# A graph network on one core: node map stored first with records of 8 words, softmax segments of 7 groups with a shorter order, and the norm product moved beside the bias product

## The reference, cut to what matters

```python
h = relu(layernorm(x))
for m in range(3):                       # block 1: attention, each node also has an edge to itself
    z = h @ W[m]; e = leaky(z[src] @ a_src[m] + z[dst] @ a_dst[m])
    w = exp(e - segment_max(e, dst)); alpha = w / segment_sum(w, dst)
    h = h + sigmoid(segment_sum(alpha * z[src], dst) + bias[m])
x = x + h
h = relu(layernorm(x)); ea = None
for l in range(3):                       # block 2: edge network
    ea = relu(concat(h[src], h[dst], ea) @ We[l] + be[l])
    h = relu(concat(h, segment_sum(ea * norm, dst)) @ Wn[l] + bn[l])
x = x + h
```

## Time and profile before

| | us |
|---|---|
| median of 3 runs | 6682.43 |
| lowest, highest | 6681.06, 6689.92 |
| profiled execution, its own time | 6695.05 |
| its span, first to last instruction | 6693.5 |
| PE busy | 4940.3 (74%) |
| DVE busy | 4362.5 (65%) |
| POOL busy | 4258.7 (64%) |
| ACT busy | 3640.2 (54%) |
| mean granted clock of PE | 0.875 |

### The profile page before, as it was taken

One profiled execution on the slowest core, in us unless ns is written; L12 is line 12 of the kernel. 1 busy time (PEld: TensorE's weight loads), 2 busy tenths in 40 slices (PEclk: granted clock), 3 DMA queues, 4 the chain that ended last, 5 costly groups with the idle time before them and its releaser, 6 DMA issues. The chain is left out here.

```text
span 6693.5 us, 109612 instructions
## 1 busy us (share of the span) xinstructions
PE 4940.3 (74%) x23142; PEld 2996.6 (45%) x23142; DVE 4362.5 (65%) x12362; ACT 3640.2 (54%) x7966; POOL 4258.7 (64%) x4317
## 2 busy tenths in 40 slices
PE   2999999999984527855782567149989997776665
PEld 1566556655651114423441445036656664333332
DVE  4887788777866747856883789855545554444443
ACT  2898889888875726643672344753323332333332
POOL 2777777777830177737745774047766665777777
PEclk9999999999998958876896555579999999999998
DMA  5788888777754536645662788877767775444442
GB/s 159 256 275 276 265 280 273 251 235 227 231 190 162 184 110 203 205 132 162 207 215 87 214 241 250 264 214 215 215 195 230 228 227 166 135 135 133 129 131 92
DMA packets 887891, 1338.57 MB, mean 200 GB/s; under 512 B 285987, under 2 KB 342895, under 8 KB 880915
## 3 DMA queue, kind: packets, MB, share of 16 engines
q1 hardware_dynamic: 744730, 1095.06, 49.2%
q0 software_dynamic: 142688, 238.37, 14.7%
HBM read 676.09 MB, written 662.90 MB: 200 GB/s over the span
## 5 line engine op out<-in xcount | busy, mean ns | idle before, releaser
L1298 POOL DMA_INDIRECT g_xs<-table,g_gi x1176 | 1205.5, 1025 | 988.9 <-DMA g_gi<-in_src_lookups_dram 404.1
L1626 POOL DMA_INDIRECT n_xs<-table,n_gi x1176 | 1202.4, 1022 | 813.7 <-DMA n_gi<-lookups 470.8
L1767 DVE TENSOR_TENSOR_SCAN n_dT<-n_km,n_dT,bank 128x512 f32<-128x512 uint8 x291 | 372.5, 1280 | 1053.5 <-PE bank L1654 1025.1
L1727 ACT ACTIVATE n_eT<-bank,edge_b 128x512 f32<-128x512 f32 x294 | 202.1, 688 | 805.4 <-PE bank L1671 805.4
L693 PE MATMUL bank<-n_zT,wn 128*128 128x512 f32 (+1 forms) x1176 | 542.7, 597 | 84.3 <-ACT n_sg L751 61.3
L674 PE MATMUL bank<-n_xT,gat_w 128*128 128x512 f32 (+1 forms) x1176 | 561.4, 615 | 54.1 <-issue 35.7
L1174 DVE CUSTOM_DVE_ANT_0 g_junk<-g_xs,v_src 128x128 f32<-128x128 f32 x1176 | 276.1, 289 | 486.8 <-DMA g_xs<-table,g_gi 486.2
L1637 POOL DMA_INDIRECT out_dram<-n_xn,n_eo x392 | 426.6, 1088 | 129.8 <-issue 114.9
L1365 PE MATMUL bank<-ident,g_xw 128*128 128x128 f32 x1176 | 240.6, 340 | 332.6 <-DVE g_acc L1193 274.7
L609 POOL DMA_INDIRECT p_rows<-in_x_dram,p_es x392 | 395.6, 1009 | 124.7 <-issue 112.3
L614 POOL DMA_INDIRECT node_map<-p_es x392 | 398.6, 1017 | 119.5 <-issue 113.4
(11 more groups left out here) (253 smaller groups left out, 12263.3 us busy)
## 6 DMA issues: line engine op xcount, KB each, us to landing
table<-n_ro SPq DMA_DIRECT2D x768, 256.0 KB
g_gb<-decays SPq DMA_DIRECT2D x294, 256.0 KB, 4.3
n_xd<-table SPq DMA_DIRECT2D x294, 256.0 KB
table<-g_xn SPq DMA_DIRECT2D x196, 256.0 KB
g_xo<-table SPq DMA_DIRECT2D x196, 256.0 KB, 4.7
edge_feats<-n_eT SPq DMA_DIRECT2D x196, 256.0 KB, 2.8
table<-n_xn SPq DMA_DIRECT2D x196, 256.0 KB, 3.1
n_ea<-edge_feats SPq DMA_DIRECT2D x196, 256.0 KB
```

The source lines that it names most:

```text
L1298: q.indirect_dma_start(out=xs[g % XR][:, u, :], out_offset=None, in_=tables[l], in_offset=bass.IndirectOffsetOnAxis(ap=gi[g % 6][:, 0, u:u ...
L1626: q.indirect_dma_start(out=xs[g][:, u, :], out_offset=None, in_=tables[L], in_offset=bass.IndirectOffsetOnAxis(ap=gi[g][:, u, slot_word:sl ...
L1767: V.tensor_tensor_scan(in_order(dT[g][:, :]), kept(g), in_order(flat_banks[1]), 0.0 if begins(g) else carry(dT[g.before(1)]), ALU.mult, AL ...
```

## The change

- Setup: records and map rows have 8 words instead of 16. DVE clears only the unused words of the records. SP issues the edge loads without waiting for DVE, except for one that loads into a tile that DVE clears first; the first node numbers are loaded ahead of them under a semaphore of their own. DVE makes the map before it takes up the edge rows, and SP stores it after the constants and before the zero rows.
- Attention layers: segments of 7 groups; two softmax functions share a step where each had one, in another order within the step; everything behind the softmax has a lag smaller by 10; XR is 20; three buffers for ACT's half sum.
- Edge layers: the norm product is a function of its own. In layers 0 and 1 it stands between `enter` and `nodes`; in layer 2 it stays behind `edges`.

```diff
@@ -27,14 +27,14 @@
 MR = UN // MG
-SG = 14
+SG = 7
 assert MAPP * MAPN == N and TP * TU == TAIL and BP * BJ == NB and BP <= P and (NM - 1) * P * MU + LP * MU == N and LP <= P and GE % SG == 0
...
 SLOPE = 0.2
-NF = 16
+NF = 8
 MW = NF
@@ -221,6 +221,7 @@
         s_mc = sem("map_cleared")
+        s_nl = sem("node_numbers_loaded")
         s_st = sem("setup_stored")
@@ -267,7 +268,7 @@
             edge_loads = [(edge_i[:, :, :], edges), (wcol[:, :], edge_w), (slots[:, :], slot_numbers),
-                          (row_i[:, :], dst_rows.rearrange("g u e -> g (u e)")), (first_numbers[:, :], node_numbers),
+                          (row_i[:, :], dst_rows.rearrange("g u e -> g (u e)")),
                           (before_i[1:GE, :], dst_rows[0:GE - 1, U - 1, P - 1:P])]
@@ -282,15 +283,28 @@
 
+                    do(V.memset(before_i[:, :].bitcast(f32), -1.0))
+                    mark["cleared"] = n[0]
                     do(V.memset(ones3[:, :], 1.0))
-                    do(V.memset(rec[:, :, :], 0.0))
+                    do(V.memset(rec[:, :, LASTM + 1:NF], 0.0))
                     do(V.memset(keep8[:, :], 0.0))
...
                     do(V.memset(negs[:, :], 0.0))
-                    do(V.memset(before_i[:, :].bitcast(f32), -1.0))
                     do(V.memset(open_first[:, :], 0.0))
                     do(V.memset(nothing[:, :, :], 0.0))
-                    mark["cleared"] = n[0]
+                    mark["unused"] = n[0]
+                    v.wait_ge(s_nl, 16)
+                    do(V.tensor_scalar(numbers[:, 0:1], first_numbers[0:MAPP, 0:1], float(MAPN // U),
+                                       -float(NODE0 * (MAPN // U - 1)), ALU.mult, ALU.add))
+                    seen()
+                    for k in range((MAPN - 1).bit_length()):
+                        m = min(1 << k, MAPN - (1 << k))
+                        do(V.tensor_scalar(numbers[:, 1 << k:(1 << k) + m], numbers[:, 0:m], float(1 << k), None, ALU.add))
+                        seen()
+                    v.wait_ge(s_mc, 1)
+                    for k in MAPPED:
+                        do(V.tensor_copy(map_rows[:, :, k], numbers[:, :]))
+                    mark["map"] = n[0]
                     v.wait_ge(s_el, 16 * len(edge_loads))
@@ -340,8 +354,6 @@
                     do(V.tensor_copy(rec_i[:, :, LASTS], slots[:, :]))
-                    do(V.tensor_scalar(numbers[:, 0:1], first_numbers[0:MAPP, 0:1], float(MAPN // U),
-                                       -float(NODE0 * (MAPN // U - 1)), ALU.mult, ALU.add))
                     seen()
@@ -359,15 +371,6 @@
                     mark["records"] = n[0]
-
-                    for k in range((MAPN - 1).bit_length()):
-                        m = min(1 << k, MAPN - (1 << k))
-                        do(V.tensor_scalar(numbers[:, 1 << k:(1 << k) + m], numbers[:, 0:m], float(1 << k), None, ALU.add))
-                        seen()
-                    v.wait_ge(s_mc, 1)
-                    for k in MAPPED:
-                        do(V.tensor_copy(map_rows[:, :, k], numbers[:, :]))
-                    mark["map"] = n[0]
 
@@ -433,13 +436,17 @@
                 def _(sp):
-                    sp.wait_ge(s_dv, mark["cleared"])
+                    sp.dma_start(first_numbers[:, :], node_numbers).then_inc(s_nl, 16)
                     for to, of in edge_loads[:-1]:
                         sp.dma_start(to, of).then_inc(s_el, 16)
+                    sp.wait_ge(s_dv, mark["cleared"])
                     with nc.allow_non_contiguous_dma("last destination of each row"):
...
                         sp.dma_start(to, of).then_inc(s_cl, 16)
+                    sp.wait_ge(s_dv, mark["map"])
+                    sp.dma_start(node_map.rearrange("(p n) w -> p n w", p=MAPP), map_rows[:, :, :]).then_inc(s_st, 16)
+                    sp.wait_ge(s_dv, mark["unused"])
                     for l in range(1, 2 * LAYERS):
@@ -455,8 +462,6 @@
                                  rec[:, :, :].rearrange("p (g u) f -> p g (u f)", u=U)).then_inc(s_st, 16)
-                    sp.wait_ge(s_dv, mark["map"])
-                    sp.dma_start(node_map.rearrange("(p n) w -> p n w", p=MAPP), map_rows[:, :, :]).then_inc(s_st, 16)
                     sp.wait_ge(s_st, 16 * (2 * LAYERS + 7))
@@ -974,7 +979,7 @@
             ends = [(S_ + 1) * SG - 1 for S_ in range(GE // SG)]
-            XR, OR = 28, 9
+            XR, OR = 20, 9
             ix, gx = sems(f"g{l}_indices_loaded", 6), sems(f"g{l}_gathered", XR)
@@ -994,7 +999,7 @@
                 xw, acc = of_ring(f"g{l}_xw", 3, c=c2), of_ring(f"g{l}_acc", 3, (C, U * P), c=c2)
-                th, xh, xn = of_ring(f"g{l}_th", 2, c=c2), of_ring(f"g{l}_xh", 2, c=c2), of_ring(f"g{l}_xn", 4, c=c2)
+                th, xh, xn = of_ring(f"g{l}_th", 2, c=c2), of_ring(f"g{l}_xh", 3, c=c2), of_ring(f"g{l}_xn", 4, c=c2)
                 xr = of_ring(f"g{l}_xr", 4, c=c2) if last_layer else None
@@ -1203,7 +1208,7 @@
                             V.scalar_tensor_tensor(out=xn[g % 4][:, :, :], in0=th[g % 2][:, :, :], scalar=0.5,
-                                                   in1=xh[g % 2][:, :, :], op0=ALU.mult, op1=ALU.add).then_inc(new, 1)
+                                                   in1=xh[g % 3][:, :, :], op0=ALU.mult, op1=ALU.add).then_inc(new, 1)
 
@@ -1211,9 +1216,9 @@
                              .then_inc(final, 1)
-                        flat(GE, [(5, source_dots), (27, add_self), (6, logits), (7, max_carry), (8, arguments), (9, sums),
-                                  (10, sum_carry), (11, shares), (12, columns), (29, sum_edges), (32, new_rows)]
-                             + ([(33, final_rows)] if last_layer else []))
+                        flat(GE, [(6, logits), (7, arguments), (8, sum_carry), (9, columns), (5, source_dots), (17, add_self),
+                                  (6, max_carry), (7, sums), (8, shares), (19, sum_edges), (22, new_rows)]
+                             + ([(23, final_rows)] if last_layer else []))
 
@@ -1282,9 +1287,10 @@
                             sp.dma_start(dots[:, g * P * U:(g + 1) * P * U], dt[g % 2][:, :]).then_inc(dl[g % 2], 16)
-                        flat(GE, [(0, load_own_scalars), (0, load_indices), (6, store_own_scalars), (14, load_scalars),
-                                  (12, store_decays), (27, load_decays), (25, load_own)]
-                             + ([(30, load_raw), (34, store_rows)] if last_layer else [(33, store_rows), (37, store_dots)]))
+                        flat(GE, [(0, load_own_scalars), (0, load_indices), (6, store_own_scalars), (8, load_scalars),
+                                  (9, store_decays), (17, load_decays), (15, load_own)]
+                             + ([(20, load_raw), (24, store_rows)] if last_layer
+                                else [(23, store_rows), (27, store_dots)]))
                         all_landed(sp, rl_, GE)
@@ -1388,9 +1394,9 @@
                                      start=True, stop=True).then_inc(dotted, 1)
-                        flat(GE, [(28, turn), (30, multiply)] + ([] if last_layer else [(33, turn_back), (35, dot)])
-                             + [(5, dots_to_rows), (6, max_to_row), (7, max_to_column), (9, sums_to_row),
-                                (10, sums_to_column), (11, to_columns)])
+                        flat(GE, [(6, max_to_row), (8, sums_to_column), (18, turn), (20, multiply)]
+                             + [(5, dots_to_rows), (6, max_to_column), (7, sums_to_row), (8, to_columns)]
+                             + ([] if last_layer else [(23, turn_back), (25, dot)]))
 
@@ -1404,8 +1410,8 @@
                             landed(a, ol, g)
-                            ready(a, new, g - 1)
-                            S.activation(xh[g % 2][:, :, :], xo[g % OR][:, :, :], ACT.Copy, bias=0.5).then_inc(half, 1)
+                            ready(a, new, g - 2)
+                            S.activation(xh[g % 3][:, :, :], xo[g % OR][:, :, :], ACT.Copy, bias=0.5).then_inc(half, 1)
 
@@ -1431,8 +1437,8 @@
                             S.activation(dt[g % 2][:, :], flat_banks[5][0:2, :], ACT.Copy).then_inc(dots_out, 1)
-                        flat(GE, [(26, scale), (31, add_half), (31, gate)]
-                             + ([] if last_layer else [(34, copy_back), (36, copy_dots)]) + [(8, weights)])
+                        flat(GE, [(7, weights), (16, scale), (20, add_half), (21, gate)]
+                             + ([] if last_layer else [(24, copy_back), (26, copy_dots)]))
             end_phase()
@@ -1669,6 +1675,8 @@
                             T.matmul(to, lhsT=we[l][:, 1, :], rhs=dT[g][:, :], start=False, stop=True).then_inc(edge, 1)
+
+                        def weights(g):
                             after(pe, msg, g, NR)
@@ -1708,9 +1716,9 @@
                         if last_layer:
-                            pipeline(pe, GE, [(4, enter), (7, last_nodes), (5, edges), (7, enter_mid), (10, turn_back)], UE)
```

(3 more changed lines are left out.)

## The result

The changed kernel takes **6509.03 us** (median of 4 runs, 6500.66 to 6529.22) beside 6686.18 for the kernel before on the same chip (4 runs, 6681.06 to 6697.49): a ratio of 0.9737, 95% interval 0.971 to 0.9765. Forecast were 6514 us and a range of 6468 to 6590. The profiled execution of the changed kernel took 6529.22 us, its span is 6527.7; before they were 6695.05 and 6693.5.

The account below looks back on a forecast made before the run. A chain of stages with barriers, each bound by its slowest resource; savings of 55 + 74 + 22 + 17 = 168 us take the profiled 6695.05 to 6527, as a median 6514, range 6468 to 6590.

Parts of the forecast that it names:

- Setup: Setup stage: node map and loads first, narrow records; ends at about 58 instead of 113 us, -55 us (-61 to -49).
- what is queued behind it there, the five zero stores and the row tables, does not feed the path: Setup, SyncE's queue behind the map's issue at about 12.5 us: claimed off the path, records issued at about 40.7.
- the backlog on five engines: Setup: map, zero stores and tables keep five DMA engines busy to about 48 us; records follow there, taking 11 us.
- Attention tails: After each attention layer's last gather: ten steps fewer at 2.8 to 3.4 us, 31 us in layers 0 and 1, 34 in the third.
- POOL's slowing: Attention layers' gathers: POOL slows when others work; 2 + 2 us in layers 0 and 1, 7 + 7 in the third.
- Edge layer 1: Norm product beside the bias product saves 0.22 us in each of 98 groups, as POOL has room: -22 us.
- Edge layer 0: Same norm product move, but POOL must follow from 5.35 to 5.13 us a group: -17 us, between -8 and -25.
- beside busy engines it took 5.26 in the attention layer, so part may be lost: Edge layer 0: POOL's free pace is 5.08 us a group, slower beside busy engines; hence -17 us.
- Stalls within the joined steps: Attention softmax: round trips to PE and ACT stall DVE; mild 6585 us, chance 0.12; strong 6711 us, chance 0.03.
- POOL one for one: Attention layers: all added DVE softmax blocks POOL for its whole length, 157 us come back, about 6660 us; chance 0.04.
- The norm product without effect: Edge layers 0 and 1: POOL paces layer 0 or PE's gaps have another cause; 6553 us, chance 0.13.
- Another transfer in the setup's way: Setup hangs on another transfer and gains only 30 us: 6539 us; within the forecast's range, no chance of its own.

Follow-up runs that it names:

- the repeat: The changed kernel timed again, nothing altered, five runs beside the kernel before: 6518.15 us, ratio 0.9736.

## Why the prediction was right, and where a step was off

*The total.* Forecast -168; the profiles differ by 165.8, the medians by 177.2 and, in the repeat, 177.7. The two forecasts of a median (6514) and of the profiled execution (6527) missed by 5 and 2 us, which is less than the runs scatter. Part of that is luck: in the pair of profiles the setup gained 4 us less than forecast and the attention layers 9 less, and the edge layers 8 more.

*Setup, -55 forecast, -51.1 measured.* The map's 25 us on five engines, its start at 12.5 (12.9) and the 11 us for the records (1.6 MB at the 147 GB/s of the row are 10.9) were right. The step that failed is "what is queued behind it there, the five zero stores and the row tables, does not feed the path". The zeros did feed it, through SP: their issue waited 29.6 us and the records behind it. The prediction had the records issued at 40.7 and their flow from 48 for another reason, the backlog on five engines. The queue brought nearly the same start, 48.75, so the wrong step cost almost nothing in the sum: with the zeros moved away from there the setup still ends at 62.7. The missing 4 us lie in the records, which flow until 61.3 and not until 58, and in the 1.4 us from there to the next stage's first load. With 80 parts, where neither cause is left, the setup ends at 54.

*Attention tails, -31, -31 and -34 forecast; -32.5, -32.1 and -35.7 measured.* Ten steps at 2.8 to 3.4 us. Fourteen groups (seven steps, 24 us) and the separate steps (three steps, 10 us) give the same price.

*POOL's slowing, +4, +4 and +14 forecast; +9.7, +12.4 and +12.7 in the pair of profiles.* Taken alone the pair says that the term was too small by half in two layers. But the gathers of one and the same attention code differ by up to 10 us from run to run: over the five kernels with the old attention layers they average 511.2, 511.7 and 540.9 us, over six with the new ones 516.6, 516.8 and 555.2. The differences are 5.4, 5.1 and 14.3. So the size was right, and a pair of profiles can't measure it. The reason given was not: the prediction let POOL slow in proportion to DVE's load. The runs show single gathers held over chains of DVE's instructions. The same doubled softmax in the old order costs 18, 24 and 25 us against the means of before (529.3, 535.8, 566.0), four to six times the forecast in the first two layers, and the order of the functions, which the prediction gave no price, brings it down to 5, 5 and 14. That the forecast of 4, 4 and 14 met this is in part luck.

*Edge layer 1, -22 forecast, -23.7 measured.* 0.22 a group was taken, 0.24 measured: one entry and one exit of 0.1, and 0.06 for the slower first f32 product behind the exit, less 0.01 between the two bf16 products.

*Edge layer 0, -17 forecast, -23.7 measured.* The step "beside busy engines it took 5.26 in the attention layer, so part may be lost" failed. POOL's pace in the middle of this layer fell to 5.10, as far as PE went. In that layer DVE is busy 309 of 528 us, against 259 of 300 in the attention layer. That POOL is less disturbed for this reason is argued; the free pace was the better row to read it from.

*The rivals.* Stalls within the joined steps: DVE waited for PE 0.2 us in 300. POOL one for one: it would have been 52 us a layer, and it is 5, 5 and 14. Single gathers do pay for a whole chain, but most of DVE's instructions meet a gather where they cost it nothing. The norm product without effect: both layers gained all of it, alone (22.7 each) as well as with the rest. Another transfer in the setup's way: the stores of zeros stood in the issue queue ahead of the records, but taking them away alone gained nothing; spreading the map over all engines gained 9 us.

## What to carry to other kernels

A store whose partition count lets it use few DMA engines leaves the others idle and holds what is queued behind it on the same issuing engine; cut it so that it spreads. Moving only what stood behind it gained nothing here. In a written-out order of steps, each step of distance between the last load and its use costs one step at the end of every layer, so a smaller segment can pay even when it doubles the fixed work, as long as that work neither paces nor slows the engine that does; count on giving part of it back. When one engine slows beside another, look at its single instructions rather than at their mean: here most gathers kept their 0.94 us and a few were held for up to 3.65. Put TensorE's short bf16 products side by side, and before a term of 5 us is judged from two profiles, look at the same stage in several kernels that share its code.

## What the runs showed that was not expected

- Stores queued behind one that uses five engines hold the issuing queue itself: 29.6 us with a map of 3.2 MB, 53.3 us with one of 6.4 MB, 6.05 us with no map ahead (the kernel with narrow rows alone). Few engines are not the only cause: behind a map on all engines it is 18.0 us, and behind the records 16.7. The Trainium skill (DMA: Bandwidth & Descriptors, How many engines) says that a transfer gets the largest number of engines up to 16 that divides the outer dimension of both its sides, which is 5 for 125 and 16 for 80. The trace agrees: a share near 0.3 with 125 parts and of 1.05 with 80.
- With full engines, packets of 128 bytes moved 147 GB/s and those of 256 bytes 218. On 16 engines that is about 14 and 19 ns a packet: half the bytes save a quarter of the time.
- POOL's gathers take 0.94 us or are held. Additions, copies and dot products of DVE hold one that begins at the wrong moment, for up to 3.65 us when they follow one another without a pause; memsets held none of 21.
- In the third attention layer 48.7 of the 56.1 us that the gathers take beyond 0.94 each lie beside one instruction, the addition of the raw rows.
- Each change between f32 and bf16 products costs TensorE about 0.1 us, and the first f32 product behind it another 0.06 to 0.10.
- Taking the joined softmax steps apart made POOL slower by 9 to 15 us a layer, with the same work: 18 gathers of the first two layers are held for over 2 us each, where it is 3 in the changed kernel.
